# A transformer stack laid out by feature on the host, with the first feed-forward weight split chunk by chunk inside the first batch

## What is computed

```python
x = x + attn_a(layernorm(x), Wqkv, Wo)            # 32 heads of 16, one key and value head, alibi, causal
x = x + ffn(layernorm(x), c1_w, c2_w, w1, w2t)
x = x + attn_b(layernorm(x), wq, wk, wv, wo)      # 32 heads of 128, 8 key heads, rope, window of 128
x = x + ffn(layernorm(x), c1_w, c2_w, w1, w2t)

def ffn(x, c1_w, c2_w, w1, w2t):                  # DIM 512, INTER 1792, blocks of 32, rank 16
    inter = x @ c1_w.T @ c2_w.T                   # the router's scores
    idx = argmax of inter within each block of 32 # one hidden unit of each block
    h = relu(w1[idx] . x)
    return h @ w2t[idx]
```

## Time and profile before

| | us |
|---|---|
| median of 3 runs | 3246.93 (3245.48 to 3249.31) |
| span of the profiled execution | 3252.0 |
| first instruction of the first and of the second feed-forward part | 770.2 and 2781.2 |
| PE, DVE, ACT, POOL busy | 2840.8, 2248.5, 1390.3, 1253.5 |

### The profile page before, as it was taken

One profiled execution on the slowest core, in us unless ns is written; L12 is line 12 of the kernel. 1 busy time (PEld: TensorE's weight loads), 2 busy tenths in 40 slices (PEclk: granted clock), 3 DMA queues, 4 the chain that ended last, 5 costly groups with the idle time before them and its releaser, 6 DMA issues. The chain is left out here.

```text
span 3252.0 us, 44782 instructions
## 1 busy us (share of the span) xinstructions
PE 2840.8 (87%) x14364; PEld 2215.5 (68%) x14404; DVE 2248.5 (69%) x4342; ACT 1390.3 (43%) x2947; POOL 1253.5 (39%) x938
## 2 busy tenths in 40 slices
PE   3798888984988896999999997799999999699888
PEld 2564545543766774788888885688888887577666
DVE  3656565644877775878787774778777787577776
ACT  2477666772322224444444443444444444232222
POOL 2266454561422222444444441444444442242221
PEclk7699988986999998999999998999999999799999
DMA  4231414224000001111010010011111100300001
GB/s 151 62 95 33 130 32 124 40 53 136 1 1 1 0 0 54 33 33 32 26 32 10 29 33 27 7 33 33 32 32 32 32 19 1 96 1 1 0 0 52
DMA packets 148429, 125.24 MB, mean 39 GB/s; under 512 B 18644, under 2 KB 117972, under 8 KB 148276
## 3 DMA queue, kind: packets, MB, share of 16 engines
q1 hardware_dynamic: 148308, 123.75, 13.7%
HBM read 96.71 MB, written 27.26 MB: 38 GB/s over the span
## 5 line engine op out<-in xcount | busy, mean ns | idle before, releaser
L1273 POOL TENSOR_TENSOR a_probs_low<-a_probs,a_probs_high 128x512 fp32r<-128x512 f32 x240 | 309.3, 1297 | 329.0 <-ACT a_probs_high L1193 328.0
L1944 POOL TENSOR_TENSOR rope_straight<-rope_straight,rope_crossed 128x512 f32<-128x512 f32 x160 | 206.9, 1293 | 477.8 <-DVE rope_crossed L1755 477.8
L634 POOL TENSOR_TENSOR f_hidden_low<-f_hidden,f_hidden_high 128x512 fp32r<-128x512 f32 x112 | 144.7, 1292 | 552.5 <-ACT f_hidden_high L579 552.5
L1049 DVE TENSOR_REDUCE a_max<-a_max_scores 128x1 f32<-128x384 f32 (+3 forms) x352 | 215.7, 637 | 153.4 <-PE a_max_scores L924 149.7
L1849 ACT ACTIVATE probs<-probs,exp_bias 128x256 f32<-128x256 f32 (+1 forms) x512 | 240.8, 471 | 168.4 <-DVE exp_bias L1737 168.1
L1596 PE MATMUL proj<-y_high,wq_high 128*128 128x512 f32 x512 | 213.3, 417 | 26.3 <-DVE y_low L1725 17.1
L1191 ACT ACTIVATE a_probs<-a_scores 128x512 f32<-128x512 f32 x320 | 192.7, 602 | 97.7 <-PE a_scores L937 48.4
L1596 PE MATMUL w_sum<-o_high,wo_high 128*128 128x512 f32 x512 | 204.2, 399 | 7.6 <-DVE xt L1779 4.7
L1910 ACT CAST probs_turned_high<-probs_turned 128x896 fp32r<-128x896 f32 x128 | 116.3, 908 | 211.9 <-PE probs_turned L1638 211.9
L1856 ACT CAST q_high<-rope_straight 128x512 fp32r<-128x512 f32 x128 | 79.5, 621 | 292.4 <-POOL rope_straight L1944 292.4
L1596 PE MATMUL proj<-y_low,wq_high 128*128 128x512 f32 x512 | 204.0, 399 | 0.0
(11 more groups left out here) (256 smaller groups left out, 8674.1 us busy)
## 6 DMA issues: line engine op xcount, KB each, us to landing
a_queries<-a_q_stacked SPq DMA_DIRECT2D x16, 1024.0 KB, 7.1
wq_raw<-in_L_attn_b_wq SPq DMA_DIRECT2D x32, 512.0 KB, 3.7
wo_raw<-in_L_attn_b_wo SPq DMA_DIRECT2D x16, 1024.0 KB, 6.2
a_q_stacked<-a_q_part_high SPq DMA_DIRECT2D x32, 256.0 KB
a_out_parts<-a_out SPq DMA_DIRECT2D x128, 64.0 KB
f_w_raw<-in_L_ffn_w SPq DMA_DIRECT2D x28, 256.0 KB, 5.3
f_w_raw<-in_L_ffn_w2t SPq DMA_DIRECT2D x14, 512.0 KB, 7.9
a_z<-a_out_parts SPq DMA_DIRECT2D x12, 512.0 KB
```

The costliest lines, as they stand in the source:

```text
L1049: e.tensor_reduce(to, scores, AX.X, ALU.max).then_inc(s["max_read"], 1)
L1273: e.tensor_tensor(pl[:, g % 4], pf[:, g % 4], f32(ph[:, g % 4]), ALU.subtract)\
L1944: e.tensor_tensor(ra[:, slot], ra[:, slot], rb[:, slot], ALU.add).then_inc(roped, 1)
```

## The change

- The host hands over x by feature (128 x 4 x 2048) and takes the output back so. `load_x` and `store_x` are gone. `causal_attention` issues the loads of the tables `eye` and `ones` and of x's first batch ahead of its own, and those of the other three batches of x behind them; `sum_x` waits for them. The second `ffn` stores each batch of `xt` from SP once it is summed, the last in four pieces; in both `ffn` the last batch's sum is in four pieces.
- The host hands over w1 transposed in 128 x 128 tiles, c1 and c2 transposed and stacked in 96 rows. Nothing is turned on PE ahead of the loop. Weights land in 14 transfers of 512 KB, w1's and w2's chunk in turn.
- w1 is split as w2 is: chunk 0 ahead of the loop, chunk c+1 in chunk c of the first batch, by ACT and POOL; w1's split stands directly ahead of w2's. `up` waits for its chunk.
- The first layer norm has its own form: the mean as four products on `xt`, the variance as four on squares that lie in the mask buffers, without POOL.
- The last batch is written out, without the preparation for a next one; the loop runs over two batches.

```diff
@@ ffn, SP @@
+            def load_weights(i):
+                two = slice(2 * i, 2 * i + 2)
+                e.dma_start(w1_raw[:, two], w1[:, two]).then_inc(w_in[i], 16)
+                e.dma_start(w2_raw[:, two], w2t[:, two]).then_inc(w_in[i], 16)
+
+            if rank is not None:
+                e.dma_start(tmp[2][:, 0:SPARSE], rank).then_inc(rank_in, 16)
+            e.dma_start(c1_raw[:, :, :], c1).then_inc(c_in, 16)
+            e.dma_start(c2_raw[:, :], c2).then_inc(c_in, 16)
             for i in range(NCH):
-                e.dma_start(w2_raw[:, 2 * i:2 * i + 2], w2v[:, 2 * i:2 * i + 2]).then_inc(w2_in[i], 16)
+                load_weights(i)
+            if out is not None:
+                for b in range(NB - 1):
+                    here = slice(b * S, (b + 1) * S)
+                    e.wait_ge(acc_added, b + 1)
+                    e.dma_start(out[:, :, here], xt[:, :, here]).then_inc(stored, 16)
+                for d in range(DT):
+                    e.wait_ge(acc_added, NB + d)
+                    e.dma_start(out[:, d, (NB - 1) * S:], xt[:, d, (NB - 1) * S:]).then_inc(stored, 16)
+                e.wait_ge(stored, 16 * (NB - 1 + DT))
...
@@ ffn, PE @@
+            def first_mean():
+                bank, full = aux_write(e, None, "mean")
+                for d in range(DT):
+                    mm = e.matmul(bank[:, :], ones[:, :], xt[:, d, 0:S], start=d == 0, stop=d == DT - 1)
+                mm.then_inc(full, 1)
+
+            def first_var():
+                bank, full = aux_write(e, None, "var")
+                for d in range(DT):
+                    e.wait_ge(first_squared, d + 1)
+                    mm = e.matmul(bank[:, :], ones[:, :], first_squares[d], start=d == 0, stop=d == DT - 1)
+                mm.then_inc(full, 1)
...
             def up(it, j):
                 e.wait_ge(h_masked, it * IT + j + 1)
+                if first_batch(it):
+                    e.wait_ge(w1_low, j // 2 + 1)
...
-                    if c == 1:
+                    if c == 1 and not last:
                         mean(it)
-                    if c == 4:
+                    if c == 4 and not last:
                         var(it)
                 down(it, IT - 2)
-                router_first(it)
+                if not last:
+                    router_first(it)
                 down(it, IT - 1)
 
             e.sem_inc(h_used, 2)
-            mean(None)
-            turn_weights(ROUTER)
-            var(None)
-            for i in range(3):
-                turn_weights(W1[i])
+            first_mean()
+            first_var()
             router_first(None)
-            turn_weights(W1[3])
-            e.wait_ge(w_low, len(jobs))
             loop(e, body)
...
@@ ffn, DVE @@
+            first_centre()
+            e.wait_ge(c_high, 1)
+            e.tensor_tensor(c1l[:, :, :], c1_raw[:, :, :], f32(c1h[:, :, :]), ALU.subtract).then_inc(c_low, 1)
             variance(None)
-            low_weights(W1[0])
+            e.wait_ge(c_high, 2)
+            rest = slice(64, CROWS)
+            e.tensor_tensor(c2s[rest, :], c2_raw[rest, :], f32(c2s[rest, :]), ALU.subtract).then_inc(c_low, 1)
             normalise(None, Chain(e, dve_step))
-            low_weights(W1[1])
             low_z(None)
-            low_weights(W1[2])
-            low_weights(W1[3])
             stack_t(None)
             loop(e, body)
-            add_out(NB - 1)
+            e.wait_ge(h_used, NB * IT + 2)
+            for d in range(DT):
+                here = xt[:, d, (NB - 1) * S:]
+                e.tensor_tensor(here, here, acc[:, d], ALU.add).then_inc(acc_added, 1)
...
@@ ffn, ACT @@
                     if first and c + 1 < NCH:
+                        high_w1(c + 1)
                         high_w2(c + 1)
...
+            e.wait_ge(c_in, 32)
+            e.copy(c1h[:, :, :], c1_raw[:, :, :]).then_inc(c_high, 1)
             for d in range(DT):
-                square(None, d)
-            high_weights(ROUTER)
+                e.wait_ge(first_centred, d + 1)
+                e.activation(first_squares[d], zf[:, d], ACT.Square).then_inc(first_squared, 1)
+            e.copy(c2s[:, :], c2_raw[:, :]).then_inc(c_high, 1)
             seed(None)
-            high_weights(W1[0])
-            high_weights(W1[1])
+            high_w1(0)
             high_z(None)
...
@@ ffn, POOL @@
                     low_hidden(it, 2 * c)
                     low_hidden(it, 2 * c + 1)
                     if first and c + 1 < NCH:
+                        low_w1(c + 1)
                         low_w2(c + 1)
...
+            def low_w1(i):
+                e.wait_ge(w1_high, i + 1)
+                e.tensor_tensor(w1l[:, 2 * i:2 * i + 2], w1_raw[:, 2 * i:2 * i + 2], f32(w1h[:, 2 * i:2 * i + 2]), ALU.subtract).then_inc(w1_low, 1)
...
-            sum_x(None, Chain(e, pool_step))
-            for n in range(3):
-                sum_squares(None, n)
+            low_w1(0)
             low_w2(0)
             loop(e, body)
@@ causal_attention, POOL and SP @@
+                if b.it is None:
+                    e.wait_ge(x_in[0], 16)
+                elif b.first:
+                    for i in range(1, NB):
+                        e.wait_ge(x_in[i], 16)
...
+            e.dma_start(ident[:, :], eye_and_ones[0]).then_inc(s["eye_in"], 16)
+            e.dma_start(ones[:, :], eye_and_ones[1]).then_inc(s["eye_in"], 16)
+            e.dma_start(xt[:, :, 0:S], x[:, :, 0:S]).then_inc(x_in[0], 16)
             e.dma_start(below_raw[:, :], after).then_inc(s["masks_in"], 16)
...
+            for b in range(1, NB):
+                here = slice(b * S, (b + 1) * S)
+                e.dma_start(xt[:, :, here], x[:, :, here]).then_inc(x_in[b], 16)
```

More of the change, by code:

```diff
@@ L49, in sem_in @@
     return lambda name: nc.alloc_semaphore(name=tag + name)
[L52 to L106, removed]
@@ L109, in store_x @@
[L109 to L150, removed]
@@ L228, in ffn @@
+        c_in, c_high, c_low = (sem(f"{tag}c_{x}") for x in ("landed", "high_ready", "low_ready"))
+        w_in = [sem(f"{tag}w_landed{i}") for i in range(NCH)]
+        w1_high, w1_low = (sem(f"{tag}w1_{x}_ready") for x in ("high", "low"))
+        w2_high, w2_low = (sem(f"{tag}w2_{x}_ready") for x in ("high", "low"))
+        first_centred, first_squared = sem(f"{tag}first_centred"), sem(f"{tag}first_squared")
+        stored, rank_in = sem(f"{tag}stored"), sem(f"{tag}rank_landed")
         aux_full = [sem(f"{tag}aux_full{i}") for i in range(2)]
@@ L252, in use, with last_batch @@
         def use(it, what, i=0):
-            n = BEFORE.index(what) if it is None else order.index((what, i)) + len(BEFORE)
+            uses = order if not last_batch(it) else [x for x in order if x[0] in "IM"]
+            n = BEFORE.index(what) if it is None else uses.index((what, i)) + len(BEFORE)
             return n % 2, (0 if it is None else it * HALF) + n // 2 + 1
+        def last_batch(it):
+            return isinstance(it, int) and it == NB - 1
         def aux_write(e, it, what, i=0):
@@ L392, in down, with body @@
                 mm.then_inc(h_used, 1)
-            def body(it, first):
+            def body(it, first, last):
                 router_scores(it, 0)
@@ L499, in body @@
                 for c in range(NCH):
-                    if c == 2:
+                    if c == 2 and not last:
                         centre(it)
-                    if c == 5:
+                    if c == 5 and not last:
                         variance(it)
@@ L589, in body @@
                         seed(it)
-                high_z(it)
-                high_t(it)
-            def high_weights(which):
-                for j in which:
-                    src, hi, _, _, _ = places(j)
-                    e.wait_ge(turned, j + 1)
-                    e.copy(hi, src).then_inc(w_high, 1)
+                if not last:
+                    high_z(it)
+                    high_t(it)
+            e.wait_ge(c_in, 32)
+            e.copy(c1h[:, :, :], c1_raw[:, :, :]).then_inc(c_high, 1)
             for d in range(DT):
-                square(None, d)
-            high_weights(ROUTER)
+                e.wait_ge(first_centred, d + 1)
+                e.activation(first_squares[d], zf[:, d], ACT.Square).then_inc(first_squared, 1)
+            e.copy(c2s[:, :], c2_raw[:, :]).then_inc(c_high, 1)
             seed(None)
-            high_weights(W1[0])
-            high_weights(W1[1])
+            high_w1(0)
             high_z(None)
-            high_weights(W1[2])
-            high_weights(W1[3])
             high_t(None)
@@ L634, in low_hidden, with body @@
                 e.tensor_tensor(hl[:, j % 2], hm[:, :], f32(hh[:, j % 2]), ALU.subtract).then_inc(hl_ready, 1)
-            def body(it, first):
-                sum_x(it, Chain(e, pool_step, it * 2 + 2))
+            def body(it, first, last):
+                if not last:
+                    sum_x(it, Chain(e, pool_step, it * 2))
                 for c in range(NCH):
```

192 lines of the change are left out of this document (81 added, 111 removed).

## The result

The changed kernel takes 3265.98 us (median of 6 runs, 3258.43 to 3270.28) where the kernel before, on the same chip, takes 3248.98 (6 runs): a ratio of 1.0047, 95% interval 1.0035 to 1.006. That is 17 us slower; the forecast was 3268.9. The profiled execution took 3267.57 us with a span of 3265.5, so the two spans differ by 13.5 us.

What follows compares the result with a forecast made beforehand. PE, busy 87% of the span, bounds the feed-forward loop, with a chain beside it next in line. Gains of 54.0 us against losses of 76.0 net +22.0 on 3246.9: 3268.9 us, range 3245 to 3285.

Steps and rivals of the forecast that it cites:

- The sign: Whole kernel: slower, net +22.0 us, because the first batch's losses exceed the gains; slower was given 0.75.
- the new wait: First batch: `up(2c+2)` waits for `w1_low`, written by POOL behind `low_hidden(2c+1)`; 5 us late at six places, period 17.15.
- the clock: First batch: PE runs slow behind each stall, 1.8 us each, six times, 10.8 per part; bounds 0 and 3.0.
- the stall: First batch: masks of chunk 6 come 29.5 us later, less 2.3 for the normalisation's multiply, 27.2 per part.
- Rival 1: First batch: w1's split is done before `up` is due, only the gains stay, 3192.9 us; 6%.
- Rival 2: First batch: stalls without a slow clock, so no change, +0.4, 3247.3 us; 20%.
- Rival 3: Slower still: 3.0 us per stall, or four-product sums at slow clock (variance at 16.5); 3277 to 3291 us; 17%.
- Rival 4: Ahead of each loop: first batch reached no earlier because router weights come late; without the 17.4 us, 3286 us; 2%.
- Start: Loading: without `load_x`, POOL's first sum waits for 1 MB of x alone and begins at 7.4; 11.3 us saved.
- Ahead of the loops: First mean to first scores: fewer POOL sums, no turned-weight casts or subtractions; 30.8 instead of 39.5 us, 8.7 saved, twice.
- Last batch: Last batch of each part: two full-precision products and the router with its stop go; 6.8 us saved, twice.
- Store: Kernel's end: four sums and a half-size store follow the last product, 6.7 instead of 19.0 us; 12.3 saved.

Runs made afterwards that it cites:

- experiment 3: Changed kernel plus products nobody reads, keeping PE busy through most of each wait for w1's split: 3243.24 us, ratio 0.9963.
- experiment 11: The changed kernel again with no edit: 3270.54 us, ratio 1.0053.
- experiment 1: Changed kernel with w1's two splits one chunk earlier (w1 of chunk c+2 in chunk c, behind w2's): 3194.72 us, ratio 0.9825.
- experiment 9: Changed kernel with w1 split one chunk earlier, POOL's later-batch sums later, last sums released by block, w1's first cast behind `high_z`: 3173.19 us, ratio 0.9747.
- experiment 4: Changed kernel with each part's last batch again preparing a next one, unread: 3289.18 us, ratio 1.0104.
- experiment 5: Changed kernel with only POOL's sum of batch 0's x back in each part's last batch, unread: 3276.65 us, ratio 1.0072.
- experiment 6: Changed kernel with w1 split one chunk earlier and POOL's sum after the first chunk's `low_hidden` in batches after the first: 3181.78 us, ratio 0.9779.

## Why the prediction was right, and where its terms were off

- **The sign** came from the new wait, and that was right in place, number and length. `up(2)` starts 20.1 us after the first scores (forecast 20.1), the masks of chunk 6 at 124.2 (113.9 and 10.8 for the clock: 124.7), the period without slow products is 17.07 (17.15). Per part the first batch lost 38.0 us; the forecast was 38.0. Behind that agreement two errors cancel: the stall costs 25.1 instead of 27.2, the clock 12.9 instead of 10.8, 2.1 per stall instead of 1.8; the price to take was the 2.1 us of the earlier trace rows, undiminished. Of the 2.1 us too many for the stall, 1.3 lie between `up(2)` and the next mask transposes: 8.0 by the forecast, 6.7 in experiment 3. That the two errors cancel was luck, the place and length of the wait were not. The Trainium skill (TensorE: Matmul & The Clock Gate, HAM oscillation) says that a loop in which PE waits long enough ahead of each tile starts every tile at the slow clock. The trace agrees in the price: behind each of the twelve stalls 7 to 14 of the 24 products of `up` and `down` are slow. It does not in the place: at `up(4)` the first six are not, though in the trace of experiment 11 they are.
- **Rival 1** (the split in time) is what experiment 1 made: 3194.7, where that rival gave 3192.9. **Rival 2** (stalls without a slow clock) is nearly what experiment 3 made: 3243.2, against 3247.3. Neither is what this change does, and the rows of the kernel before decided rightly between them. **Rival 3** asked for 3.0 us per stall and for a variance at 16.5 us; the runs gave 2.1, and 13.1 and 12.3. **Rival 4** falls too: the first scores of each part came 7 us sooner after its start.
- **Start:** 10.6 saved, 11.3 forecast; x landed 0.5 us later.
- **Ahead of the loops:** counted from the part's first instruction, 7.1 saved in part 1, with 0.3 lost elsewhere in that stretch, and 7.7 in part 2, where 8.7 each were forecast. The variance was in at 12.3 us in part 2 (12.5), and the router's products took 4.6 (5.4). What failed is the sentence that w1's first split lies "on POOL under the normalisation" as if that were free: it held the third step for 2.0 us (experiment 9).
- **Last batch:** the step that failed most. 6.8 per part were forecast; the traces give 12.4 in part 1 and 10.8 in part 2, and experiment 4 gives 23 in all. Three things were not in the term: POOL's sum for the batch after the next, which held `low_z` for 3.2 us (experiment 5); the router's products, which I priced from the last batch of part 2 with its full clock (2.9 us), while in part 1 of the kernel before they took 4.3, mostly at the slow one; and 0.8 us ahead of them, which I only argue: the normalisation's multiply held `keep_hidden` in the last chunk, and PE waited 0.36 us for `low_hidden` there. I had read rows of PE and asked which of its instructions go. The question left out was which instruction on POOL goes, and whom it held up. The rows had it: PE waits 5.42 us for `low_z` in the earlier trace rows and 2.22 in the earlier trace rows, and the 3.2 us between the two are POOL's sum. I read them as two lengths of idleness and did not ask why one was longer.
- **Store:** 13.1 saved, 12.3 forecast.
- **The sum:** +22.0 forecast, +13.5 between the two traces, 17 between the medians. The 8.5 us of difference between forecast and traces are the last batch (-9.6), the two stretches ahead of the loops (+2.6), the start (+0.7), the store (-0.8), window attention with the sum ahead of it (-1.7, of which I traced no cause), and causal attention (+0.3). The closeness of 3268.9 to 3266.0 owes something to chance as well: the forecast stands on the 3246.9 of three runs, and six gave 3249.0, so of a step of 22 us 17 were measured.

## What to carry to other kernels

Work that is spread over a loop to save a stage must be placed by its due time: the same split of 2.5 us cost 0.2 to 0.4 us one chunk earlier and 6 us where it stood behind the last link of a chain. If an added instruction is needed by the next step, look for what its engine still waits for at that moment, not for how busy it is. And when a change removes work from POOL or adds some, look at what DVE does in that window; in these kernels four kinds of DVE operation were held up by POOL's, each at a place where PE waited for what came behind it.

## What the runs showed of the hardware

- **DVE and POOL exclude each other in some operations.** Beside a POOL split or sum, DVE's [128x512] step took 2.71 instead of 0.69 us, four `low_z` 6.37 instead of 3.17, c2's split 3.86 instead of 2.02, a mask write 2.00 to 2.04 instead of 0.69. The step in the timeline ahead of the first loop ended 0.54 us after POOL's split, as if it had only begun when that ended, while L334, which was already running when POOL's split began, kept its 0.69. The mask write of experiment 1 (795.28) ended 0.54 us after POOL's as well, and the reduction ahead of it (L360, one input), which began and ended within that split, kept its 0.69. The Trainium skill says so (SBUF — State Buffer, Who interferes with whom): a DVE operation with two inputs in SBUF and a POOL operation that reads it take turns, and whichever issues first holds the port for its whole length. The rows agree. I had not weighed that rule when I costed the change.
- **The same idle time gave either clock.** In the kernel before, at the same place in the last batch, the router's first four products took 2.02 us in part 1 and 1.17 in part 2; the forecast's "after 2.22 us nothing was lost" was the second of these alone:

```profile
1216.56 2.02 PE L348 MATMUL f_aux<-f_z_high,f_c_high 128*96 128x512 f32 x4 [2.23 <-DVE f_z_low L455]
```

So it is in the other kernels: 1.16 us after a wait of 2.22 in experiment 6 (998.22), 1.94 after 2.25 in the changed kernel (1134.34). After 3.89 us (832.63) the first six products of `up(4)` still ran 0.23 to 0.31 us apart, and the slow ones came behind them, at 0.43. So the length of one wait doesn't say which products are slow. The sum over a batch was steady: what the first batch's products lost against a spacing of 0.23 us came to about 12 us in each part of the changed kernel, 13 in its second trace, and to 4 to 4.6 in the kernel before.
